# A GNN kernel on one core: VectorE's one-hots for pair n are weighed during pair n+1, and the chain that makes a row is spread over the steps of a half

## What is computed

```python
h = jnp.maximum(_layernorm(x, axis=-1), 0.0)
msg = edge_val[:, None] * h[src]
neighbor = jax.ops.segment_sum(msg, dst, num_segments=6250)
out = neighbor @ W1.T + b1 + (h * neighbor) @ W2.T + b2
x = x + jax.nn.leaky_relu(out, negative_slope=0.2)
h = jnp.maximum(_layernorm(x, axis=-1), 0.0)
agg = jax.ops.segment_sum(h[src], dst, num_segments=6250)
```

## Time and profile before

| | us |
|---|---|
| Runs | 2548.17, 2548.80, 2556.46 (median 2548.8) |
| Profiled execution, its own time | 2543.86 |
| Its span, first to last instruction | 2542.2 |
| PE busy in the span | 2208.5 (87%) |
| DVE busy | 1629.0 (64%) |
| ACT busy | 1240.5 (49%) |
| Mean granted clock | 0.942 |

### The profile page before, as it was taken

One profiled execution on the slowest core, in us unless ns is written; L12 is line 12 of the kernel. 1 busy time (PEld: TensorE's weight loads), 2 busy tenths in 40 slices (PEclk: granted clock), 3 DMA queues, 4 the chain that ended last, 5 costly groups with the idle time before them and its releaser, 6 DMA issues.

```text
span 2542.2 us, 59418 instructions
## 1 busy us (share of the span) xinstructions
PE 2208.5 (87%) x20122; PEld 1970.1 (77%) x20167; DVE 1629.0 (64%) x3146; ACT 1240.5 (49%) x3113; POOL 130.1 (5%) x107
## 2 busy tenths in 40 slices
PE   1699999999999999999995899899998426999897
PEld 1499999999999999999995667667887416888644
DVE  8688888888888888888886555655774682000133
ACT  4555555555555555555552666677886310000142
POOL 6300000000000000000000000000001340000000
PEclk6699999999999999999998899999999758999999
DMA  8122121212112121212121432333583238888221
GB/s 250 57 80 88 60 87 59 88 59 80 67 66 81 60 87 60 87 59 88 59 84 43 172 110 109 112 116 124 214 311 110 57 114 305 300 301 301 86 69 53
DMA packets 186973, 299.45 MB, mean 118 GB/s; under 512 B 15753, under 2 KB 139020, under 8 KB 186804
## 3 DMA queue, kind: packets, MB, share of 16 engines
q1 hardware_dynamic: 183664, 287.55, 33.2%
q0 software_dynamic: 3248, 11.13, 1.5%
HBM read 198.15 MB, written 100.49 MB: 117 GB/s over the span
## 4 chain that ended last, share of the span: by engine, by line
PE 41%; DVEq 30%; DVE 13%; issue 9%; DMA 3%; ACT 2%; ACTq 1%; POOL 0%; POOLq 0%; SPq 0%; PEldq 0%
PE ps L898 20%; DVEq L1602 14%; DVEq L1605 11%; PE ps L882 5%; PE ps L806 4%; PE ps L795 3%; PE ps L868 3%; PE ps L1019 2%; PE ps L789 2%; DVE edge_area L1603 1%; DVE edge_area L1600 1%; DVE hT_s L1462 1%; DVEq L1600 1%; DMA hs<-node_rows 1%; PE ps L938 1%
## 5 line engine op out<-in xcount | busy, mean ns | idle before, releaser
L1153 ACT CAST edge_area<-ps 128x392 f16<-128x392 f32 x784 | 387.3, 494 | 559.4 <-PE ps L789 559.4
L806 PE MATMUL ps<-big,rows_area 128*128 128x128 f32 x4802 | 572.4, 276 | 0.0
L806 PEld LDWEIGHTS ps<-big,rows_area 128*128 128x128 f32 x4802 | 552.8, 192 | 0.0
L795 PE MATMUL ps<-edge_area 128*128 128x196 f16 x4704 | 540.8, 249 | 0.0
L795 PEld LDWEIGHTS ps<-edge_area 128*128 128x128 f16 x4704 | 421.2, 97 | 0.3
L1159 ACT COPY big<-ps 128x392 f32<-128x392 f32 x784 | 387.5, 494 | 13.0 <-PE ps L795 1.5
L789 PE MATMUL ps<-edge_area 128*128 128x196 f16 x2352 | 335.7, 250 | 59.5 <-DVEq L1605 58.7
L1601 DVE TENSOR_TENSOR edge_area<-cell_pair,carry 128x1176 f16<-128x1176 f16 x392 | 299.8, 765 | 0.0
L898 PE MATMUL ps<-big,agg 128*128 128x256 f16 (+1 forms) x2450 | 288.4, 277 | 0.0
L898 PE MATMUL ps<-big,rows_area 128*128 128x256 f16 (+1 forms) x2450 | 264.6, 272 | 24.9 <-DMA big<-edge_counts 24.9
L1600 DVE TENSOR_TENSOR edge_area<-lo_pair,carry 128x768 f16<-128x768 f16 x392 | 218.9, 559 | 97.2 <-issue 85.9
(11 more groups left out here) (235 smaller groups left out, 1809.6 us busy)
## 6 DMA issues: line engine op xcount, KB each, us to landing
big<-edge_counts SPq DMA_DIRECT2D x336, 448.0 KB, 4.9
edge_counts<-edge_area SPq DMA_DIRECT2D x49, 1568.0 KB, 5.9
hs<-node_rows POOLq DMA_DIRECT2D x14, 448.0 KB, 4.6
edge_area<-x_stream SPq DMA_DIRECT2D x14, 448.0 KB, 3.9
node_rows<-rows_area SPq DMA_DIRECT2D x1, 3136.0 KB, 12.5
agg_s<-node_rows SPq DMA_DIRECT2D x49, 64.0 KB, 5.2
agg_s<-in_x SPq DMA_DIRECT2D x49, 64.0 KB, 4.8
x_stream<-agg_s SPq DMA_DIRECT2D x49, 64.0 KB, 1.7
```

Source lines behind the costliest of these rows:

```text
L795: last = mm(group_of(p_weight[s % 4], c), weights_of(oh, slot, r, c), cells_of(slot, r, c), start=(c == 0 and oh is oh_whi), stop=(c == 2 ...
L806: last = mm(p_sum, h0[:, n, :], w32[:, par, n, :], start=(n == 0), stop=(n == NB - 1))
L1153: nc.scalar.copy(store_slot[:, par, :, cols], p_count[s % 2]).then_inc(sem("count_taken"), 1)
```

## The change

One-hots: a step j now makes the two comparisons of pair j and then the two products of pair j-1, with no drain between them, and one drain ends the step. `onehots` is raised by the last product itself, so for pair j in step j+1. After the loop the last pair is weighed alone.

Row chain: it is cut into its operations, and a step gets one or two of them ahead of its drain, from different rows: in half h steps 0 to 5 and 7 carry bias, leaky, sum, statistics, mean, epsilon and reciprocal of row h-3, steps 0 to 2 carry normalising, relu with high plane, and low plane of row h-4; `prod1` moves from step 5 to step 6. ScalarE takes the square root behind supergroup 9, not 3. SP's store of the h row is a half later than that of the x row, and the load of an x row waits for a new semaphore, `x1_read`, that the normalising raises. Halves 3 and 4 are now written out too; the loop starts with half 5. The tail has one more half row to do, and SP's order in it differs.

```diff
@@ -432,9 +432,11 @@
                 sp.wait_ge(sem("x1_in"), g * 16 + 16)
                 sp.sem_inc(sem("passed"), 1)
+                sp.wait_ge(sem("x1_read"), g + 1)
+                sp.sem_inc(sem("passed"), 1)
                 sp.dma_start(x_row[par], row_of(A["x"], g)).then_inc(sem("x1_in"), 16)
-            def store_rows(g, par):
+            def store_x(g, par):
                 sp.wait_ge(sem("x1_out"), g * 16 + 32)
                 sp.sem_inc(sem("passed"), 1)
@@ -442,6 +444,8 @@
                 sp.sem_inc(sem("passed"), 1)
                 sp.dma_start(row_of(x_dram, g), x_row[par]).then_inc(sem("x1_out"), 16)
+            def store_h(g, par):
+
                 sp.wait_ge(sem("h1_out"), g * 16 + 32)
                 sp.sem_inc(sem("passed"), 1)
                 sp.wait_ge(sem("h1_new"), g + 1)
@@ -469,10 +474,12 @@
                 sp.sem_inc(sem("half_saved0"), 16)
                 sp.sem_inc(sem("half_saved1"), 16)
-                def half(h, b, par):
+                def half(h, b, par, older=True):
                     load_h_row(h - 1, 1 - par)
                     load_x_row(h - 2, par)
-                    store_rows(h - 3, 1 - par)
+                    store_x(h - 3, 1 - par)
+                    if older:
+                        store_h(h - 4, par)
                     store_half(h, b, par)
                 store_half(0, 0, 0)
@@ -481,21 +488,27 @@
                 load_h_row(1, 1)
                 load_x_row(0, 0)
                 store_half(2, 1, 0)
-                with sp.Fori(1, NHALF // 2) as i:
+                half(3, 1, 1, False)
+                half(4, 2, 0)
+                with sp.Fori(2, NHALF // 2) as i:
                     half(i * 2 + 1, i, 1)
                     half(i * 2 + 2, i + 1, 0)
                 load_h_row(NB - 1, 0)
                 load_x_row(NB - 2, 1)
-                store_rows(NB - 3, 0)
+                store_x(NB - 3, 0)
+                store_h(NB - 4, 1)
                 load_x_row(NB - 1, 0)
-                store_rows(NB - 2, 1)
+                store_x(NB - 2, 1)
+                store_h(NB - 3, 0)
+                store_x(NB - 1, 0)
+                store_h(NB - 2, 1)
                 sp.wait_ge(sem("deg_counted"), 1)
                 sp.dma_start(deg_dram.rearrange("o (g p j) -> p (o g) j", g=NGT, p=P), deg_g[:]).then_inc(
                     sem("deg_out"), 16)
                 sp.dma_start(inv_deg_dram.rearrange("o (g p j) -> p (o g) j", g=NGT, p=P), inv_deg_g[:]).then_inc(
                     sem("deg_out"), 16)
-                store_rows(NB - 1, 0)
+                store_h(NB - 1, 0)
                 sp.wait_ge(sem("deg_out"), 32)
                 sp.wait_ge(sem("half_saved0"), 16 * (NHALF // 2 + 1) + 16)
                 sp.wait_ge(sem("half_saved1"), 16 * (NHALF // 2) + 16)
@@ -552,6 +565,7 @@
             sp.sem_inc(sem("h_in1"), 16)
             sp.sem_inc(sem("x1_in"), 16)
+            sp.sem_inc(sem("x1_read"), 2)
             sp.sem_inc(sem("x1_out"), 32)
             sp.sem_inc(sem("h1_out"), 32)
             branch(sp, order, both(edges_any(0), rows_any), count_sorted)
@@ -1174,7 +1188,7 @@
                     take_supergroup(h, par, i, s)
                     if s == 0 and summed:
                         take_sum(h - 2, par)
-                    if s == 3 and normed:
+                    if s == 9 and normed:
                         row_std(h - 3)
             def count_sorted():
@@ -1593,17 +1607,18 @@
             def paired(iota, n):
                 return iota[:].rearrange("p (o n) e -> p o n e", o=1).to_broadcast([P, 3, n, 2])
-            def duo_onehots(duo, slot):
+            def make_onehots(duo, slot):
                 dve.wait_ge(sem("weight_ready"), duo * 2 + 2)
-                key, lo, whi, wlo = (t[:, bass.ds(duo * 3, 3), :, :] for t in by_duo)
+                key, lo = (by_duo[n][:, bass.ds(duo * 3, 3), :, :] for n in (KEY, LO))
                 V.tensor_tensor(oh_src[:, slot], paired(lo_pair, P), lo.to_broadcast([P, 3, P, 2]), ALU.is_equal)
                 V.tensor_tensor(oh_cell[:, slot], paired(cell_pair, CELLS), key.to_broadcast([P, 3, CELLS, 2]), ALU.is_equal)
-                dve.drain()
+
+            def weigh_onehots(duo, slot):
+                whi, wlo = (by_duo[n][:, bass.ds(duo * 3, 3), :, :] for n in (WHI, WLO))
                 V.tensor_tensor(oh_whi[:, slot], oh_src[:, slot], whi.to_broadcast([P, 3, P, 2]), ALU.mult)
-                V.tensor_tensor(oh_wlo[:, slot], oh_src[:, slot], wlo.to_broadcast([P, 3, P, 2]), ALU.mult)
-                dve.drain()
-                dve.sem_inc(sem("onehots"), 1)
+                V.tensor_tensor(oh_wlo[:, slot], oh_src[:, slot], wlo.to_broadcast([P, 3, P, 2]), ALU.mult).then_inc(
+                    sem("onehots"), 1)
             def prod1(g, par):
                 dve.wait_ge(sem("hT1"), g + 3)
@@ -1611,50 +1626,111 @@
                 dve.wait_ge(sem("sum_taken"), g + 2)
                 V.tensor_tensor(prod_one, p_rowT, sum_s[par], ALU.mult).then_inc(sem("prod1"), 1)
-            def new_x(g, par):
+            def add_bias1(g):
                 dve.wait_ge(sem("lin1"), g + 3)
                 V.tensor_tensor(lin_one, p_lin, bias1[:], ALU.add).then_inc(sem("lin1_read"), 1)
-                dve.drain()
+
+            def leaky():
                 V.scalar_tensor_tensor(out=lin_one, in0=lin_one, scalar=SLOPE, in1=lin_one, op0=ALU.mult, op1=ALU.max)
-                dve.drain()
+
+            def add_x(g, par):
                 dve.wait_ge(sem("x1_in"), g * 16 + 32)
                 V.tensor_tensor(x_row[par], x_row[par], lin_one, ALU.add).then_inc(sem("x1_new"), 1)
-                dve.drain()
+
+            def row_stats(par):
                 V.bn_stats(stats[:, 0, :], x_row[par])
-                dve.drain()
+
+            def row_mean():
                 V.bn_aggr(mv[:, 0, :], stats[:, 0, :])
-                dve.drain()
+
+            def row_var():
                 V.tensor_scalar(rstd[:, 0:1], mv[:, 0, 1:2], EPS, None, ALU.add).then_inc(sem("ln_var"), 1)
-            def new_h(g, par):
+            def row_rstd(g):
                 dve.wait_ge(sem("ln_std"), g + 2)
                 V.reciprocal(rstd[:, 0:1], rstd[:, 0:1])
-                dve.drain()
-                V.tensor_scalar(norm_one, x_row[par], mv[:, 0, 0:1], rstd[:, 0:1], ALU.subtract, ALU.mult)
-                dve.drain()
+
+            def row_norm(par):
+                V.tensor_scalar(norm_one, x_row[par], mv[:, 0, 0:1], rstd[:, 0:1], ALU.subtract, ALU.mult).then_inc(
+                    sem("x1_read"), 1)
+
+            def halves_of(g):
+                return (planes1[:, bass.ds(g, 1), n, :].rearrange("p o n -> p (o n)") for n in range(2))
+
+            def row_relu(g, par):
                 dve.wait_ge(sem("h1_out"), g * 16 + 16)
                 V.tensor_scalar(new_row[par], norm_one, 0.0, None, ALU.max).then_inc(sem("h1_new"), 1)
-                hi, lo = (planes1[:, bass.ds(g, 1), n, :].rearrange("p o n -> p (o n)") for n in range(2))
+                hi, _ = halves_of(g)
                 V.tensor_scalar(hi, norm_one, 0.0, SCALE, ALU.max, ALU.mult)
-                dve.drain()
+
+            def row_rest(g, par):
+                hi, lo = halves_of(g)
                 V.scalar_tensor_tensor(out=lo, in0=new_row[par], scalar=SCALE, in1=hi, op0=ALU.mult,
                                        op1=ALU.subtract).then_inc(sem("planes_ready1"), 1)
-            def half_onehots(h, par, rows=True, older=True):
+            def half_onehots(h, par, summed=True, last=True, oldest=True, first=False):
+
                 for j in range(DUOS):
-                    duo_onehots(h * DUOS + j, j % RING)
-                    if older and j == 1:
-                        new_x(h - 3, 1 - par)
-                    if rows and j == 5:
+                    make_onehots(h * DUOS + j, j % RING)
+                    if not (first and j == 0):
+                        weigh_onehots(h * DUOS + j - 1, (j - 1) % RING)
+                    if oldest:
+                        if j == 0:
+                            row_norm(par)
+                        if j == 1:
+                            row_relu(h - 4, par)
+                        if j == 2:
+                            row_rest(h - 4, par)
+                    if last:
+                        if j == 0:
+                            add_bias1(h - 3)
+                        if j == 1:
+                            leaky()
+                        if j == 2:
+                            add_x(h - 3, 1 - par)
+                        if j == 3:
+                            row_stats(1 - par)
+                        if j == 4:
+                            row_mean()
+                        if j == 5:
+                            row_var()
+                        if j == 7:
+                            row_rstd(h - 3)
+                    if summed and j == 6:
                         prod1(h - 2, par)
-                    if older and j == 6:
```

(59 more changed lines are left out.)

## The result

| | changed kernel | before |
|---|---|---|
| Median of the runs shown with the result, us | 2483.0 (2477.8 to 2484.3, 4 runs) | 2548.5 (4 runs) |
| Profiled execution, its own time | 2483.87 | 2543.86 |
| Its span | 2482.2 | 2542.2 |

The ratio is 0.9733, 95% interval 0.9708 to 0.9758: faster, by 65 us. The forecast was 2480, in a range from 2468 to 2502.

What follows compares the result with a forecast made beforehand. VectorE was taken to bound the counting loop, with PE next. Loop -68.2, tail -2.1 and +1.9 sum to -68.4: 2543.86 becomes 2475.5, and with 4.9 for the median 2480 us, range 2468 to 2502.

Steps and rivals of the forecast that it cites:

- The bound and the floor: Counting loop: VectorE sets 25.82 us per half; after the change PE sets 24.23, 68.2 us less over 47 halves.
- The one-hots' drain: VectorE, between compare and weighing: without the drain the products start 0.68 after the comparison, a pair costs 2.53 instead of 2.78.
- The row chain: VectorE's twelve small row operations per half: 2.1 to 3.4 us, 2.5 taken; VectorE's whole half then 22.9.
- The waits: VectorE's new waits, for PE's `lin1` in step 0 and ScalarE's square root in step 7: 3 and 2.5 us to spare.
- The lags worked out for step 7: Reciprocal waits for the square root, pair 7's weighing behind it: announced 2.2 us after pair 5, wanted at 4.7, 2.5 to spare.
- rival 3: Slower: the wait for `lin1` in step 0 starves PE each half, 26.93 us per half, 2608 us; 4%.
- The wait of step 0: Bias waits for PE's `lin1`, pair 0's weighing unannounced behind it; 3 us to spare before PE wants pair 0.
- The tail: After the last pair: earlier degree counting gains 3.4 us, one more `row_planes` costs 1.3, net -2.1; later degree stores +1.9.
- the term for SP's wait: Tail: degree stores go 1.9 us later, and the next stage's loads stand behind SP's wait: +1.9, 0 to +3.
- The 4.9 us: Added to 2475.5 because the median of the old kernel's three runs, 2548.8, lay 4.9 above its profiled execution.

Runs made afterwards that it cites:

- b1: Kernel before with 12 of the 49 weighting products of a half left out: 2547.0 us, 25.86 us per half.
- e3: Changed kernel with 6 of the 49 weighting products of a half left out: 2419.4 us, 22.89 us per half.
- e1: Kernel before with only the one-hots' new order; row chain and order on SP and ScalarE as before: 2472.3 us, ratio 0.9703.
- e2: Changed kernel with each pair's own weighing and the drain before it put back, so only the row chain's part: 2476.6 us, ratio 0.9720.
- e5: Changed kernel with ScalarE's square root behind supergroup 11 instead of 9: 2491.5 us in one run, 24.23 us per half.
- e7: Changed kernel with SP's two degree stores put back ahead of the last rows' stores in the tail: 2478.75 us, ratio 0.9742 to before.
- e6: Changed kernel with ScalarE's square root behind supergroup 13 instead of 9: 2773.4 us, 30.4 us per half.
- e8: Changed kernel with the four degree-counting passes moved from the tail to behind halves 1 to 4, degree stores behind half 4: 2469.7 us, ratio 0.9702 to before.
- e9: Changed kernel with each degree-counting pass cut in four pieces, in steps 2 to 5 of halves 1 to 4: 2473.1 us, ratio 0.9688 to before.

## Why the prediction was right, and where it was off

**The bound and the floor.** Right, and by the number: 24.23 us read off the first halves of the old trace was the rate of all 47 in the new one, 68.1 us against 68.2. b1 and e3 show both bounds, each by leaving out PE's work.

**The one-hots' drain.** 0.93 to 0.68 between L1615 and L1619, as worked out. A plain step comes to 2.49 (e1: 2.49 to 2.50 between comparisons), against 2.53.

**The row chain.** The term was too high: the half came to 22.1, not 22.9. With 8 x 2.49 and 0.15 the twelve operations cost 2.0 us, just under the 2.1 that I had as the lower bound; almost nothing of their waits and addresses is exposed. As PE set the rate, this moved no time. But the prediction summed the two parts and never asked what each is worth alone. e1 and e2 show that either would have done. For the one-hots alone its own numbers said so: with the whole of today's 3.43 for the rows it had 23.8, under 24.23. For the rows alone they did not: 8 x 2.78 + 0.15 + 2.1 = 24.5 at the least. That part sufficed because a pair costs less than taken, 2.49 + 0.25, and so do the rows, 2.0: 24.1 in all with the 0.15.

**The waits.** At their places and small (1.0 and 0.9 us a half). The lags worked out for step 7 were good: 1.6 us later costs nothing (e5), 6.3 us later makes PE stand still 3.6 (3.8 expected). The mechanism of rival 3, one-hots made but not announced behind a wait, is thus real: behind the wait of step 7 it lies 6.3 - 3.6 = 2.7 us away from this kernel, and it is dearer than its idle time, for the clock falls with it. The wait of step 0, the one that rival 3 named, was moved in no run.

**The tail.** -2.1 and +1.9 became -3.5 and +1.6. The counting started earlier than expected (5.6 us ahead of the last run, not 4.8) and the planes added 0.6, not 1.3. Taking the later stores back brought 4.6 (e7), so they cost more than the term for SP's wait.

**What was not in the sum.** The last stage, +7.3 us in the profiled execution, from TensorE's clock, and 3.1 us ahead of VectorE's first comparison. Sum -68.4, span -60.0; the medians differ by 65.5. So the 3 us between the forecast of 2480 and the median of 2483.0 are in part luck. For the profiled execution the sum gave 2475.5, and it took 2483.9, 8.4 more. The 4.9 us that the prediction added, because the old profiled execution lay that far under its median, made up for more than half of it; the new one lies 0.9 above its median.

## What to carry to other kernels

When an engine sets a loop's rate, look for a stretch of the same trace in which it did not, because of a lead: the rate there is the floor, and no edit to the first engine gets below it. Then price each part of an edit against that floor alone; here either part reached it, and the whole change ran 12 us slower than the one-hots' part alone. Of the 9.4 us that the two profiles show of this, 3.2 are a longer tail; most of the rest is a slower last stage, whose cause is open. The slack that is left on the engine that waits now is the next thing to spend: moving the tail's counting into it gave 15 us more.

## What the runs showed of the hardware that I had not expected

Pauses of 3.4 to 3.8 us in an otherwise full TensorE, once every 30 us, brought its granted clock to 0.89 on the mean and cost another 2.9 us each, nearly all by the slower clock (e6). With pauses of up to 1.0 us it stayed at 1.00 (before, 700 to 1269 us), with pauses of up to 2.0 us it was 0.97 (b1, 300 to 1250 us). VectorE's idle time before its first instruction of the next stage, named issue by the profile, took 2.8 to 3.2 us, and 5.6 to 7.2 where two stores of 26 KB were in flight (e7, e8, e9 against the other eleven). Behind a pause of 3.6 to 4.1 us, the last stage of an unchanged TensorE program averaged 0.85, 0.70 or 0.52 of the clock over its first 20 us, and the moment at which the clock had fallen, 0.8 to 1.9 us ahead of the first matmul, put all fourteen profiles in these three groups.
